# A windowed-attention block on one core: DVE, ACT and GpSimd do a step's work in another order

## The chip, the cores and the metric

The kernel runs on one core of one Trainium2 chip. The metric is the device time of one launch in microseconds (us), taken as the median of several runs. The kernel has five instruction streams: PE (matmul, with its weight loads shown apart as PEld), DVE (vector), ACT (scalar), POOL (GpSimd) and SP (which here only issues DMAs).

## What is computed

A Swin-like block over a float32 image batch of shape (4, 256, 256, 96), rolled by (-4, -4) and cut into 8x8 windows of 64 tokens. The reference, cut to what matters:

```
h = _ln(win, ln1_g, ln1_b)
q = jnp.einsum('ntc,chd->nthd', h, wq) + bq
k = jnp.einsum('ntc,chd->nthd', h, wk) + bk
v = jnp.einsum('ntc,chd->nthd', h, wv) + bv
scores = jnp.einsum('nqhd,nkhd->nhqk', q, k) * (1.0 / np.sqrt(KD))
attn = jax.nn.softmax(scores, axis=-1)
o = jnp.einsum('nhqk,nkhd->nqhd', attn, v)
win = win + jnp.einsum('nqhd,hdc->nqc', o, wo) + bo
h2 = _ln(win, ln2_g, ln2_b)
win = win + jax.nn.gelu(h2 @ w1 + b1, approximate=False) @ w2 + b2
```

There are 3 heads of 32 channels, and `_ln` is a layer norm over the 96 channels.

## The kernel before

**Tiling and stages.** The image is cut into 256 units of 1024 tokens (half a row of windows each). Sixteen units make a batch, and there are 16 batches. A batch is an attention stage of 16 steps and then an MLP stage of 16 units. Every unit stays in SBUF in `stream` from its load to its store.

**An attention step is a software pipeline over units.** In PE's step s (PE `attention_step`) these follow each other: the scores of unit s+1 (L645), the three transposes of unit s's probabilities, one per head (L660), the first half of the q and k projections of unit s+2 (L612, six matmuls), the product of probabilities and values (L675), the second half of q and k (L612), v (L629), and the output projection of unit s (L688). PE takes its instructions in order, so one that waits holds all behind it.

**The other engines in the same step.** DVE takes the row maxima (L1017) and subtracts them (L1024) head by head, sums the exponentials (L1032) and inverts the sums (L1040), all for unit s+1. Then it adds the attention output into `stream` (L1046) and takes the eight `bn_stats` of unit s for the second layer norm (L963, `statistics2`). ACT copies the transposed probabilities (L810), takes three exponentials (L821), copies q and k (L800, L804), o (L827) and v (L815) out of PSUM, and rounds each half of the normalised input of unit s+3 to fp32r (L792, `copy_hT_upper`). POOL subtracts that rounded half from the input to get the lower part (L398, `copy_hT_lower`), and multiplies the exponentials by the inverse sums (L391, `normalise_probs`, three instructions, one per head).

**What sets the order.** Each engine's order is written out by hand, and semaphores join them. POOL's step was: lower half 0, the three products, lower half 1, with statistics work (`finish1`, `finish2`: nine or ten small instructions), `normalise2` or `lower_early` ahead of it in some steps. The products of POOL's step s are read by the transposes of PE's step s+1, and the lower halves of POOL's step s are read by the q and k projections of the same PE step s+1: the first matmul there waits for half 0.

**The way of the normalised input.** ACT normalises unit u (`normalise1`, L781), DVE transposes it in blocks (`turn_h1`, L1010), SP sends it to DRAM (L301) and fetches it back in another layout (L309) for `copy_hT_upper`. SP waits in order: in its step s it sends unit s+4 and then fetches unit s+3. In batch 0 every step does this. In the later batches three steps do, and the rest of it falls into the MLP stage, except the fetch, which every step has.

Of the kernel before, what the change touches and what calls it, by code (L numbers as in the profile page):

```python
# [42 lines left out]
BATCH = 16  # L43
# [11 lines left out]
AHEAD = 3  # L55
# [13 lines left out]
def swin_block(nc, x, ln1_g, ln1_b, wq, bq, wk, bk, wv, bv, wo, bo, ln2_g, ln2_b, w1, b1, w2, b2, out):  # L69
# [3 lines left out]
    with ExitStack() as ctx:  # L73
# [306 lines left out]
        def _(pool):  # L380
# [146 lines left out]
            def attention(b):  # L527
                batch = b * BATCH
                call = LN_CALLS * (b - 1) + BATCH_0_CALLS
                for s in range(BATCH):  # L530
# [20 lines left out]
                    if s == 13:  # L551
                        lower_early(b, batch + 1, 1, copy_h2T_early(batch + 1, 1))
                    copy_hT_lower(batch + s + 3, (s + 3) % 2, 0)
                    normalise_probs(batch + s + 1, (s + 1) % 2)
# [214 lines left out]
        def _(act):  # L769
# [62 lines left out]
            def attention_step(u, half):  # L832
# [8 lines left out]
                if not absent(front):  # L841
                    copy_qk(front, 0)
                    copy_qk(front, 1)
                if not absent(middle):
                    exps(middle, 1 - half, 1)
# [5 lines left out]
                copy_hT_upper(u + 3, 1 - half, 0)  # L851
# [91 lines left out]
        def _(dve):  # L943
# [149 lines left out]
            def attention_step(u, half):  # L1093

                back, middle = u, u + 1
                if not absent(middle):
                    for h in range(HEADS):
                        maxima(middle, h)
                        shift(middle, 1 - half, h)
                    for h in range(HEADS):  # L1100
                        sums(middle, 1 - half, h)
                    invert_sums(middle)
                if not absent(back):
                    for g in range(2):
                        add_attention(back, g)

            def first_attention():

                for s in range(-5, BATCH):
                    if s >= -AHEAD:  # L1110
                        attention_step(s, s % 2)
                    if s >= 0:
                        statistics2(s, s)
# [3 lines left out]
                    if s + 8 < BATCH + AHEAD + 1:  # L1117
                        first_statistics(s + 8)
                    if s + 5 < BATCH + AHEAD:
                        turn_h1(s + 5, turned1_early)  # L1120
                    if s in (6, 8, 12):
                        n = (6, 8, 12).index(s)
                        turn_h2(n, turned_early, n == 0)

            TURNS1 = (9, 11, 13)
            TURNS2 = (5, 8, 10)

            def attention(b):
                batch = b * BATCH

                def whole_step(s):
                    attention_step(batch + s, s % 2)
                    statistics2(batch + s, s)

                wait_apart(dve, h1_left, 16 * (batch + BATCH))
                with dve.Fori(0, 1):
                    for s in range(6):
                        whole_step(s)
                        if 2 <= s < 3 + AHEAD:
                            n = s - 2  # L1140
                            statistics1(batch + BATCH + n, n, b * BATCH_ROWS + BATCH_ROWS + n // 2, n % 2)
                        if s == TURNS2[0]:
                            turn_h2(batch, turned_early, True)
                with dve.Fori(3, 4) as r:
                    for half in (0, 1):
                        attention_step(batch + 2 * r + half, half)
                        statistics2(batch + 2 * r + half, 2 * r + half)
                with dve.Fori(0, 1):
                    for s in range(8, 14):
                        whole_step(s)  # L1150
# [3 lines left out]
                        if s in TURNS2:  # L1154
                            n = TURNS2.index(s)
                            turn_h2(batch + n, turned_early, False)
                with dve.Fori(7, 8) as r:
                    for half in (0, 1):
                        attention_step(batch + 2 * r + half, half)
                        statistics2(batch + 2 * r + half, 2 * r + half)  # L1160
# [65 lines left out]
```

## Time and profile before

| what | value |
|---|---|
| median of 3 runs | 5030.46 us (5025.09 to 5032.2) |
| the profiled execution | 5033.9 us |
| its span, first to last instruction | 5029.7 us |
| mean granted TensorE clock | 0.998 |
| PE / PEld / DVE / ACT / POOL busy | 95% / 78% / 82% / 79% / 78% |

The views used are the page of the profile, the list of waits (who waited for whom, in total), and the timeline (instructions of an engine in order of time, runs of the same line merged into one row with their count). The timeline's times are us from the start of the span. A row starts with its start and its duration, and a bracket at its end is the idle time of the engine ahead of it and what ended that.

### The profile page before, as it was taken

To read this page: it belongs to the slowest core of one execution; us is meant where nothing else is said; L and a number is where in the kernel's file an instruction comes from. 1 tells how busy PE (TensorE), PEld (TensorE's weight loads), DVE (VectorE), ACT (ScalarE), POOL (GpSimd) and SP (SyncE) were. 2 spreads that over 40 slices of the span, in tenths; PEclk is the share of its full clock that TensorE was granted. 3 is DMA by queue.
4 is the path that set the end of the run, shared out by engine and by line. 5 is a ranking of instruction groups with operands and counts; after the bars stand their busy time and mean duration, and the time that the engine had idled before them with its cause. 6 is when DMAs were issued, how large, how long until landed. Compare 5 with 4: busy or idle time off the path is not lost.

```text
span 5029.7 us, 290167 instructions
## 1 busy us (share of the span) xinstructions
PE 4792.6 (95%) x109308; PEld 3899.6 (78%) x109308; DVE 4101.5 (82%) x9010; ACT 3953.4 (79%) x8309; POOL 3913.3 (78%) x4457
## 2 busy tenths in 40 slices
PE   5899999999999999999999999999999999999999
PEld 4687777878778787787877878778787777878777
DVE  7887878788787887878878788787887878888787
ACT  6887878777787777878778777787887878877787
POOL 6796868878687886878868688686896868878687
PEclk9999999999999999999999999999999999999999
DMA  4443443533434343343433434334343443533334
GB/s 124 116 160 94 124 136 93 171 96 123 128 101 161 95 138 117 103 160 97 138 112 109 155 91 150 105 117 148 101 154 95 127 135 97 168 99 123 126 100 163
DMA packets 374740, 622.61 MB, mean 124 GB/s; under 512 B 38761, under 2 KB 241226, under 8 KB 374282
## 3 DMA queue, kind: packets, MB, share of 16 engines
q1 hardware_dynamic: 372720, 618.28, 39.5%
q14 instruction: 449, 3.68, 0.2%
q10 hardware_dynamic: 1562, 0.50, 0.1%
q8 instruction: 9, 0.15, 0.0%
HBM read 310.35 MB, written 308.28 MB: 123 GB/s over the span
## 4 chain that ended last, share of the span: by engine, by line
PE 39%; DVE 16%; issue 14%; POOL 13%; ACT 8%; DMA 4%; SPq 3%; DVEq 3%; ACTq 0%; POOLq 0%
PE psum L722 12%; PE psum L736 11%; POOL probs L391 6%; PE psum L612 6%; DVE stats L963 4%; PE psum L629 3%; DVE normed L1067 3%; POOL rstd L430 2%; POOL hT_lower L398 2%; PE psum L688 2%; DVE stream L1046 2%; PE psum L675 2%; SPq L276 2%; DVE normed L1060 2%; DMA h_raw_odd<-turned_rows 2%
## 5 line engine op out<-in xcount | busy, mean ns | idle before, releaser
L781 ACT ACTIVATE normed<-stream,shift,rstd 128x96 f32 (+1 forms) x2176 | 809.8, 458 | 254.0 <-DVE probs L1010 241.2
L1046 DVE TENSOR_TENSOR stream<-stream,psum 128x384 f32 (+1 forms) x1024 | 562.8, 550 | 467.9 <-PE psum L736 226.5
L430 POOL TENSOR_TENSOR rstd<-variance,minus_half 128x16 f32<-128x16 f32 (+1 forms) x265 | 791.7, 2988 | 20.8
L398 POOL TENSOR_TENSOR hT_lower<-h_raw_odd,hT_upper 96x512 fp32r<-96x512 f32 x258 | 329.8, 1278 | 595.0 <-ACT hT_upper L792 591.1
L391 POOL TENSOR_TENSOR probs<-probs,prob_inv 128x512 f32<-128x512 f32 x771 | 781.8, 1040 | 0.0
L810 ACT ACTIVATE gelu_odd<-psum 128x512 f32<-128x512 f32 x768 | 424.4, 596 | 431.6 <-PE psum L660 426.0
L963 DVE BATCH_NORM_STATS2 stats<-stream 128x6 f32 (+2 forms) x4224 | 714.1, 243 | 42.0 <-DVE stream L1046 36.3
L821 ACT ACTIVATE probs<-probs 128x512 f32<-128x512 f32 x771 | 486.8, 631 | 122.7 <-DVE probs L1024 122.6
L736 PEld LDWEIGHTS psum<-w_w,gelu_odd 128*64 128x64 f32 x12288 | 511.2, 137 | 58.6 <-issue 58.6
L1024 DVE TENSOR_TENSOR probs<-psum,row_max 128x512 f32<-128x512 f32 x771 | 533.3, 692 | 26.6
L1032 DVE TENSOR_REDUCE prob_sum<-probs 128x8 f32<-128x512 f32 x771 | 492.0, 678 | 76.0 <-ACT probs L821 75.2
L736 PEld LDWEIGHTS psum<-w_w,gelu_even 128*64 128x64 f32 x12288 | 511.3, 137 | 51.2 <-issue 51.2
L736 PE MATMUL psum<-w_w,gelu_odd 128*64 128x96 f32 x12288 | 535.2, 247 | 12.2 <-ACT gelu_odd L865 12.2
L398 POOL TENSOR_TENSOR hT_lower<-h_raw_even,hT_upper 96x512 fp32r<-96x512 f32 x260 | 332.4, 1279 | 270.9 <-ACT hT_upper L792 269.9
L736 PE MATMUL psum<-w_w,gelu_even 128*64 128x96 f32 x12288 | 535.2, 247 | 3.3
L660 PE MATMUL psum<-ident,probs 128*128 128x128 f32 x3072 | 463.0, 284 | 78.5 <-POOL probs L391 59.4
L1017 DVE TENSOR_REDUCE row_max<-psum 128x8 f32<-128x512 f32 x771 | 521.1, 676 | 15.9 <-PE psum L645 15.8
L865 ACT ACTIVATE gelu_odd<-psum 128x512 f32<-128x512 f32 x768 | 428.6, 591 | 120.0 <-PE psum L722 93.3
L487 POOL TENSOR_TENSOR stream<-stream,b_all 128x768 f32 (+1 forms) x256 | 487.1, 1906 | 26.3 <-POOL rstd L430 25.3
L865 ACT ACTIVATE gelu_even<-psum 128x512 f32<-128x512 f32 x768 | 425.5, 590 | 79.5 <-PE psum L722 54.7
L612 PE MATMUL psum<-hT_upper,qk_split_upper 128*96 128x512 f32 x1032 | 449.9, 436 | 26.6 <-POOL hT_lower L398 23.0
L660 PEld LDWEIGHTS psum<-ident,probs 128*128 128x128 f32 x3072 | 325.4, 141 | 181.3 <-issue 163.0
(99 smaller groups left out, 11188.3 us busy)
## 6 DMA issues: line engine op xcount, KB each, us to landing
turned_rows<-probs SPq DMA_DIRECT2D x416, 384.0 KB, 2.4
h_raw_odd<-turned_rows SPq DMA_DIRECT2D x242, 384.0 KB, 3.9
stream<-in_x SPq DMA_DIRECT2D x272, 192.0 KB, 3.6
h_raw_even<-turned_rows SPq DMA_DIRECT2D x130, 384.0 KB
out<-stream SPq DMA_DIRECT2D x256, 192.0 KB
stream<-in_x SPq DMA_DIRECT2D x272, 180.0 KB
out<-stream SPq DMA_DIRECT2D x256, 180.0 KB
oT<-turned_rows SPq DMA_DIRECT2D x112, 384.0 KB
```

The source lines that it names most:

```text
L391: nc.gpsimd.tensor_tensor(block_h, block_h, inv, ALU.mult).then_inc(probs_ready, 1)
L398: nc.gpsimd.tensor_tensor(lower[:, tokens], h_raw[parity][0:C, tokens], upper[:, tokens], ALU.subtract).then_inc(hT_copied, 1)
L430: nc.gpsimd.tensor_tensor(flat(rstd), variance[:, 0:n], minus_half[:, 0:n], ALU.pow)\
L612: last = nc.tensor.matmul(psum[0:C, QK_BANKS[n], :], qk_split[w][:, which, :], hT_split[h][:, group * SHARES:(group + 1) * SHARES], start= ...
L660: last = nc.tensor.transpose(psum[:, PT_BANKS[h], quad * P:(quad + 1) * P], probs[:, buffer, h, 2 * quad:2 * quad + 2, :].rearrange("p a k ...
L722: last = nc.tensor.matmul(psum[:, UP_BANKS[part][j], :], w1_split[w][:, j * P:(j + 1) * P], h2T[parity][h][:, part * SHARES:(part + 1) * S ...
L736: last = nc.tensor.matmul(psum[WT * side:WT * (side + 1), DOWN_BANKS[part], t * C:(t + 1) * C], gelu[parity][:, j, c * P + WT * side:c * P ...
L781: last = nc.scalar.activation(normed1[:, t, :], stream[:, slot, t * C:(t + 1) * C], ACT.Identity, bias=shift1[:, index, t:t + 1], scale=rs ...
L865: nc.scalar.activation(in_rows[:, 2 * part:2 * part + 2, :, :], psum[:, UP_BANKS[part][j], :].rearrange("p (b t i) -> p b t i", b=2, i=BLOCK),
L963: last = nc.vector.bn_stats(stats[:, index, c, :], stream[:, slot, c * C:(c + 1) * C])
L1024: nc.vector.tensor_tensor(probs[:, buffer, h, :, :], psum[:, S_BANKS[h], :].rearrange("p (t k) -> p t k", k=WT), row_max[:, h, :].unsqueez ...
L1046: nc.vector.tensor_tensor(part, part, psum[:, banks[g], 0:GROUP], ALU.add).then_inc(added, 1)
```

## The change

DVE: `statistics2` of a unit leaves the end of its step and stands in the next step between the second and the third sum. The work that was done after it in some steps (`statistics1`, `turn_h1`, `turn_h2`) now stands behind the inversion and ahead of the two additions. In batch 0 the `statistics1` moves in this way and `turn_h1` and `turn_h2` stay at the step's end. The fourth `statistics1` of a batch moves from step 5 to step 6. ACT: `copy_hT_upper` of half 0 moves from behind the third exponential to behind the first two copies of q and k. POOL: the three products move ahead of lower half 0. The loops of DVE are cut in other places. Nothing is added or removed.

```
--- before.py
+++ after.py
@@ -550,8 +550,8 @@
                         finish2(call + 5, batch + 6, 6, 2)
                     if s == 13:
                         lower_early(b, batch + 1, 1, copy_h2T_early(batch + 1, 1))
+                    normalise_probs(batch + s + 1, (s + 1) % 2)
                     copy_hT_lower(batch + s + 3, (s + 3) % 2, 0)
-                    normalise_probs(batch + s + 1, (s + 1) % 2)
                     copy_hT_lower(batch + s + 3, (s + 3) % 2, 1)
                 return call + 6
 
@@ -841,6 +841,7 @@
                 if not absent(front):
                     copy_qk(front, 0)
                     copy_qk(front, 1)
+                copy_hT_upper(u + 3, 1 - half, 0)
                 if not absent(middle):
                     exps(middle, 1 - half, 1)
                 if not absent(back):
@@ -848,7 +849,6 @@
                     copy_oT(back, 1)
                 if not absent(middle):
                     exps(middle, 1 - half, 2)
-                copy_hT_upper(u + 3, 1 - half, 0)
                 if not absent(front):
                     copy_qk(front, 2)
                     copy_qk(front, 3)
@@ -1090,16 +1090,22 @@
                 dve.wait_ge(down_done, 2 * u + g + 1)
                 add_into_stream(u, DOWN_BANKS, g, mlp_added)
 
-            def attention_step(u, half):
+            def attention_step(u, half, index, extra=()):
 
                 back, middle = u, u + 1
                 if not absent(middle):
                     for h in range(HEADS):
                         maxima(middle, h)
                         shift(middle, 1 - half, h)
-                    for h in range(HEADS):
-                        sums(middle, 1 - half, h)
+                    sums(middle, 1 - half, 0)
+                    sums(middle, 1 - half, 1)
+                if not (isinstance(index, int) and index < 1):
+                    statistics2(u - 1, index - 1)
+                if not absent(middle):
+                    sums(middle, 1 - half, 2)
                     invert_sums(middle)
+                for work in extra:
+                    work()
                 if not absent(back):
                     for g in range(2):
                         add_attention(back, g)
@@ -1108,56 +1114,48 @@
 
                 for s in range(-5, BATCH):
                     if s >= -AHEAD:
-                        attention_step(s, s % 2)
-                    if s >= 0:
-                        statistics2(s, s)
+                        extra = [lambda: first_statistics(s + 8)] if s + 8 < BATCH + AHEAD + 1 else []
+                        attention_step(s, s % 2, s, extra)
+                    else:
+                        first_statistics(s + 8)
                     if s == -4:
                         for halves in h2T:
                             constant_rows(*halves)
-                    if s + 8 < BATCH + AHEAD + 1:
-                        first_statistics(s + 8)
                     if s + 5 < BATCH + AHEAD:
                         turn_h1(s + 5, turned1_early)
                     if s in (6, 8, 12):
                         n = (6, 8, 12).index(s)
                         turn_h2(n, turned_early, n == 0)
-
+                statistics2(BATCH - 1, BATCH - 1)
+
+            STATS1 = (2, 3, 4, 6)
             TURNS1 = (9, 11, 13)
             TURNS2 = (5, 8, 10)
 
             def attention(b):
                 batch = b * BATCH
 
-                def whole_step(s):
-                    attention_step(batch + s, s % 2)
-                    statistics2(batch + s, s)
-
-                wait_apart(dve, h1_left, 16 * (batch + BATCH))
-                with dve.Fori(0, 1):
-                    for s in range(6):
-                        whole_step(s)
-                        if 2 <= s < 3 + AHEAD:
-                            n = s - 2
+                def step(s):
+
+                    def extra():
+                        if s in STATS1:
+                            n = STATS1.index(s)
                             statistics1(batch + BATCH + n, n, b * BATCH_ROWS + BATCH_ROWS + n // 2, n % 2)
-                        if s == TURNS2[0]:
-                            turn_h2(batch, turned_early, True)
-                with dve.Fori(3, 4) as r:
-                    for half in (0, 1):
-                        attention_step(batch + 2 * r + half, half)
-                        statistics2(batch + 2 * r + half, 2 * r + half)
-                with dve.Fori(0, 1):
-                    for s in range(8, 14):
-                        whole_step(s)
                         if s in TURNS1:
                             n = TURNS1.index(s)
                             turn_h1(batch + BATCH + n, turned1_early)
                         if s in TURNS2:
                             n = TURNS2.index(s)
-                            turn_h2(batch + n, turned_early, False)
-                with dve.Fori(7, 8) as r:
-                    for half in (0, 1):
-                        attention_step(batch + 2 * r + half, half)
-                        statistics2(batch + 2 * r + half, 2 * r + half)
+                            turn_h2(batch + n, turned_early, n == 0)
+
+                    attention_step(batch + s, s % 2, s, (extra,))
+
+                wait_apart(dve, h1_left, 16 * (batch + BATCH))
+                for part in (range(0, 6), range(6, 11), range(11, BATCH)):
+                    with dve.Fori(0, 1):
+                        for s in part:
+                            step(s)
+                statistics2(batch + BATCH - 1, BATCH - 1)
 
             def mlp(b):
                 batch_row = b * BATCH_ROWS
```

**DVE in batch 0**, from the additions of one step to the inversion of the next (`gelu_even` is the buffer that `turn_h1` writes). Before:

```order
L1046 TENSOR_TENSOR stream<-stream,psum 128x384 x2
L963 BN_STATS stats<-stream 128x6 x16
L1010 STREAM_TRANSPOSE gelu_even<-normed 128x8x24x4
L1017 TENSOR_REDUCE row_max<-psum 128x8
...
L1024 TENSOR_TENSOR probs<-psum,row_max 128x512
L1032 TENSOR_REDUCE prob_sum<-probs 128x8 x3
L1040 RECIPROCAL prob_inv<-prob_sum 128x24
```

Now:

```order
L1046 TENSOR_TENSOR stream<-stream,psum 128x384 x2
L1010 STREAM_TRANSPOSE gelu_even<-normed 128x8x24x4
L1017 TENSOR_REDUCE row_max<-psum 128x8
...
L1024 TENSOR_TENSOR probs<-psum,row_max 128x512
L1032 TENSOR_REDUCE prob_sum<-probs 128x8 x2
L963 BN_STATS stats<-stream 128x6 x8
L1032 TENSOR_REDUCE prob_sum<-probs 128x8
L1040 RECIPROCAL prob_inv<-prob_sum 128x24
L963 BN_STATS stats<-stream 128x6 x8
```

Eight of the sixteen `bn_stats` went between the sums, and eight behind the inversion. In the later batches the eight of `statistics2` do the same.

**POOL at the start of a later batch's attention.** Before:

```order
L398 TENSOR_TENSOR hT_lower<-h_raw_odd,hT_upper 96x512
L387 REGISTER_ALU
L391 TENSOR_TENSOR probs<-probs,prob_inv 128x512 x3
L397 REGISTER_ALU
L398 TENSOR_TENSOR hT_lower<-h_raw_odd,hT_upper 96x512
```

Now:

```order
L391 TENSOR_TENSOR probs<-probs,prob_inv 128x512 x3
L397 ISA
L398 TENSOR_TENSOR hT_lower<-h_raw_odd,hT_upper 96x512
L397 REGISTER_ALU
L398 TENSOR_TENSOR hT_lower<-h_raw_odd,hT_upper 96x512
```

The three products went ahead of lower half 0, and both halves now follow the third product.

**ACT in one step of batch 0**, from the copies of the transposed probabilities to the normalisation. Before:

```order
L810 ACTIVATE gelu_odd<-psum 128x512 x3
L821 ACTIVATE probs<-probs 128x512
L800 ACTIVATE qT<-psum 96x128x4
L804 ACTIVATE kT<-psum 96x16x32
L821 ACTIVATE probs<-probs 128x512
L827 ACTIVATE oT<-psum 96x8x16x4 x2
L821 ACTIVATE probs<-probs 128x512
L792 ACTIVATE hT_upper<-h_raw_odd 96x512
```

Now:

```order
L810 ACTIVATE gelu_odd<-psum 128x512 x3
L821 ACTIVATE probs<-probs 128x512
L800 ACTIVATE qT<-psum 96x128x4
L804 ACTIVATE kT<-psum 96x16x32
L792 ACTIVATE hT_upper<-h_raw_odd 96x512
L821 ACTIVATE probs<-probs 128x512
L827 ACTIVATE oT<-psum 96x8x16x4 x2
L821 ACTIVATE probs<-probs 128x512
```

The rounding of half 0 went ahead of two exponentials and two copies. PE's and SP's orders are unchanged.

## Rows read from the trace of the kernel before

**Rows 1.** The page: busy time of each engine.
```profile
PE 4792.6 (95%) x109308; PEld 3899.6 (78%) x109308; DVE 4101.5 (82%) x9010; ACT 3953.4 (79%) x8309; POOL 3913.3 (78%) x4457
```

**Rows 2.** Waits of all engines: us in total, times, longest us.
```profile
POOL hT_lower L398 <- ACT hT_upper L792: 861.0, 222, 23.0
...
PE psum L660 <- POOL probs L391: 59.4, 174, 1.6
...
ACT hT_upper L792 <- DMA h_raw_odd<-turned_rows: 30.9, 44, 5.1
```

**Rows 3.** Timeline of PE, step 1 of batch 4: start, duration, instruction.
```profile
1328.13 0.89 PE L645 MATMUL psum<-kT,qT 32*64 32x64 f32 x61
...
1330.82 0.47 PE L612 MATMUL psum<-hT_upper,qk_split_upper 128*96 128x512 f32 x1
...
1332.06 0.40 PE L612 MATMUL psum<-hT_lower,qk_split_upper 128*96 128x512 f32 x1
...
1338.00 1.29 PE L645 MATMUL psum<-kT,qT 32*64 32x64 f32 x96
```

**Rows 4.** Timeline of PE: batch 4's first scores, and its MLP's first matmul.
```profile
1318.27 0.97 PE L645 MATMUL psum<-kT,qT 32*64 32x64 f32 x67 [0.42 <-issue]
...
1488.04 0.47 PE L722 MATMUL psum<-h2T_even_upper,w_split_upper 128*128 128x512 f32 x1
```

**Rows 5.** Timeline of PE, a step of batch 4: third transposes, first q projection.
```profile
1405.23 0.65 PE L660 MATMUL psum<-ident,probs 128*128 128x128 f32 x4 [0.35 <-POOL probs L391]
...
1405.70 0.44 PE L612 MATMUL psum<-hT_upper,qk_split_upper 128*96 128x512 f32 x1
```

**Rows 6.** Timeline of POOL, the same step.
```profile
1402.07 3.03 POOL L391 TENSOR_TENSOR probs<-probs,prob_inv 128x512 f32<-128x512 f32 x3
...
1405.07 1.27 POOL L398 TENSOR_TENSOR hT_lower<-h_raw_even,hT_upper 96x512 fp32r<-96x512 f32 x1
```

**Rows 7.** Timeline of ACT, the same step.
```profile
1407.41 0.58 ACT L804 ACTIVATE kT<-psum 96x512 f32<-96x512 f32 x1
...
1407.89 0.63 ACT L821 ACTIVATE probs<-probs 128x512 f32<-128x512 f32 x1
...
1409.43 0.62 ACT L821 ACTIVATE probs<-probs 128x512 f32<-128x512 f32 x1
1409.95 0.62 ACT L792 ACTIVATE hT_upper<-h_raw_odd 96x512 fp32r<-96x512 f32 x1
1410.47 0.59 ACT L800 ACTIVATE qT<-psum 96x512 f32<-96x512 f32 x1
```

**Rows 8.** Timeline of DVE, the same step.
```profile
1403.12 1.38 DVE L963 BATCH_NORM_STATS2 stats<-stream 128x6 f32 x8 [0.15 <-DVE stream L1046]
...
1408.38 1.27 DVE L1032 TENSOR_REDUCE prob_sum<-probs 128x8 f32<-128x512 f32 x2
...
1410.08 0.69 DVE L1032 TENSOR_REDUCE prob_sum<-probs 128x8 f32<-128x512 f32 x1 [0.43 <-ACT probs L821]
...
1410.80 0.30 DVE L1040 RECIPROCAL prob_inv<-prob_sum 128x24 f32<-128x24 f32 x1
```

**Rows 9.** Timeline of batch 0: PE's scores 13 steps apart (first and last row), normalisation to rounding.
```profile
61.49 1.54 PE L645 MATMUL psum<-kT,qT 32*64 32x64 f32 x96 [3.09 <-issue]
...
158.38 2.99 ACT L781 ACTIVATE normed<-stream,shift,rstd 128x96 f32<-128x96 f32 x8
...
161.40 0.98 DVE L1010 STREAM_TRANSPOSE gelu_even<-normed 128x768 f32<-128x768 f32 x1 [0.36 <-ACT normed L781]
...
163.02 0.35 SPq L309 DMA_DIRECT2D h_raw_odd<-turned_rows  x1
...
167.33 0.63 ACT L792 ACTIVATE hT_upper<-h_raw_odd 96x512 fp32r<-96x512 f32 x1
...
218.34 1.28 PE L645 MATMUL psum<-kT,qT 32*64 32x64 f32 x96 [0.79 <-ACT v L815]
```

**Rows 10.** Windows, batch 0: us; busy PE, PEld, DVE, ACT, POOL; granted clock; DMA.
```profile
220.00:225.00 5.00, 3.11 (x15) 2.37 (x16) 3.12 (x5) 3.60 (x9) 5.00 (x6) 0.78 0.25 79
```

## Prediction

> **What bounds the kernel now.** The page first [rows 1]: PE is busy for 95% of the span, so that a faster order has at most the last few per cent of it to win, and all other engines have about a fifth of their time free. In such a kernel the question is which chain holds PE up inside a step. The MLP stage has the same instructions in the same order after the change, so I read the attention steps alone.
>
> The list of waits [rows 2] shows PE's third transposes waiting for POOL's products 174 times, 59.4 us in all. POOL itself waited 861 us for ACT's rounded half before it could do the lower half. Both are what the change moves. So next the timeline of PE in one step. Step 1 of batch 4 [rows 3] runs without a wait: scores at 1328.13, the first q projection at 1330.82 (2.69 later), the next scores at 1338.00, which is a step of 9.87 us. From the first q projection to the next scores it is 7.18 us. Call the moment of that first projection Q. A step then lasts (Q measured from its scores) + 7.18, and nothing is won below 9.87.
>
> The whole attention stage of batch 4 goes from 1318.27 to 1488.04 [rows 4], 169.8 us for 16 steps, 10.61 a step. The most that the change can win is therefore 0.74 x 16 = 11.9 us a batch, 190 us in all. In a later step of it [rows 5, 6] POOL's third product ends at 1405.10, the third transposes start 0.13 later, and Q is 0.47 behind them: Q is 0.60 after the end of the third product. I call that end E.
>
> **The change, part by part.**
>
> *POOL's order.* The products no longer stand behind a lower half that takes 1.27 [rows 6]. But PE's first q projection needs that lower half, and in the same PE step as the products. It now starts at E - 0.03 and ends at E + 1.24, and with the handoff of 0.13 Q is at E + 1.37 in place of E + 0.60. So the products come up to 1.2 us earlier and 0.77 of it goes into a new wait of PE, at L612 on L398. What is queued behind the waiting matmul is all of the step that is left.
>
> *ACT's order.* The rounding of half 0 starts 0.52 ahead of what follows it (1409.95 to 1410.47) [rows 7], so the second and third exponentials come 0.52 later after the copies of q and k.
>
> *DVE's order.* The eight `bn_stats` take 1.38 [rows 8] and no longer stand ahead of the maxima, which now start when the scores are done. That is worth nothing once the chain of the exponentials, which runs through ACT, ends later than the subtractions. Between the second and third sum they cost what they exceed DVE's wait there: it was 0.43 of idle time [rows 8], and with both exponentials late by the same amount some 0.4 of the `bn_stats` stay uncovered. The other moved work (`statistics1`, the turns) goes into the time after the inversion, where DVE waits for the output projection. I cost it at nothing: it has about a microsecond of room there, and if that is gone the additions, and with them the transposes that need their banks, come late by tenths.
>
> *The new loop.* These close into a loop from E of one step to E of the next. In us after E:
> - Q at 1.37, as above.
> - Six matmuls to the end of the last, 1332.06 + 0.40 - 1330.82 = 1.64 [rows 3], and about 0.03 of handoff, as from an exponential's end at 1410.05 to its sum at 1410.08 [rows 7, 8]: the copy of k starts at 3.04.
> - The rounding 0.48 later (3.52), the second exponential 0.52 after that (4.04), 0.63 long, handoff 0.03: its sum at 4.70.
> - The next DVE instruction starts 0.59 later, since two sums take 1.27 and not 1.36. The `bn_stats` start at 5.29 and let the third sum start, overlapped in the same way, at 6.59.
> - The third exponential is ready before that: four ACT starts behind the rounding, 2.06 less the 0.04 overlaps, its end is near 6.1. So the third sum waits for DVE, not for ACT.
> - Inversion 0.72 later, 0.30 long [rows 8]: 7.61.
> - Handoff to POOL, which no row shows: between 0.03 and 0.13. I take 0.10, between the two. Three products, 3.03 [rows 6]: E again after **10.75 us**.
>
> In the loop nothing has slack, so the step is 10.75 wherever it has settled. Between the end of lower half 1 (two halves after E, 2.5) and the next products (7.7) POOL has 5.2 us in which its statistics work lies hidden; if it should not fit, six steps of a batch are late by tenths, which the bounds take in. The normalisations of three steps of a batch, 3 us of ACT each, stay hidden as far as ACT waits for the transposes anyway; I cost them at nothing, and if that cover is gone they too are tenths.
>
> *A later batch.* Step 0 starts with everything ready, 9.87. Its own inversion has no `bn_stats` in it, so step 1 is about 10.5. Fourteen of 10.75 are 150.5. Sum 170.9, against 169.8: **+1.1 us**, times 15 batches **+17 us**. The steps that were longest before (with sixteen `bn_stats` ahead of the maxima) get shorter, and the plain ones get longer. For the bounds: if the handoffs and overlaps of the loop are 0.2 shorter it is -25 us, if 0.25 longer +70.
>
> *Batch 0.* Here every step has a second loop: normalisation (2.99), turn (starts 161.40), then SP sends, then fetches (163.02), and the rounding starts at 167.33, 4.3 after the fetch [rows 9]. In this batch ACT reached the rounding only a moment before the data, and steps are (218.34 - 61.49) / 13 = 12.07 us. Now ACT comes to the rounding 2.06 us earlier in its order (1407.89 to 1409.95) [rows 7], but the data are no earlier, since SP's fetch stands behind a send that waits for the turn. ACT stands still with two exponentials and two copies behind it, and these 2.06 us then lie between the rounding and the next normalisation. The loop becomes 14.1. Fourteen steps of it: **+29 us**. The bounds are nothing (the fetch lands in time after all) and the same again.
>
> [...]
>
> **Sum.** 5033.9 + 17 + 29 = 5080 for an execution like the profiled one. That one was 3.4 above the median of the runs, so 5076 is the forecast.
>
> **The rivals.**
>
> *A. Faster: PE does not wait for the lower half.* If E comes early enough in the step (1.32 or less after the scores, so that Q stays at 2.69), the earlier maxima decide. It needs the inversion 0.9 us earlier than my loop gives from an undisturbed Q. For it speaks that DVE starts the maxima up to 1.3 us earlier, and that PE waited for POOL 174 times. Against it, the second exponential stands on ACT behind the copy of k, which no earlier maximum moves. With steps of 10.0, a batch is 160, -9.8 x 15 = -147, and with batch 0's +29 the median is 4912. In a half form (a loop of 10.5, and half of batch 0's cost) it is 5033.9 - 36 + 15 - 3.4 = 5010. The two together 0.16.
>
> *B. Batch 0 costs nothing*, because the fetch lands before ACT gets there: 5047. Against it, ACT already waited for that DMA 44 times [rows 2]. 0.08.
>
> *C. The clock.* PE will wait nearly a microsecond in each step (10.75 - 9.87). In batch 0 the granted clock was 0.78 in the mean of a stretch of 5 us in which PE was busy for only 3.11 of them [rows 10], so at half its rate for 2.2 us, which loses about 1.1. One such dip in every fifth of 15 x 14 steps would give 42 x 1.1 = +46, near 5122, and one in every second step +115, near 5190. Against it, the mean granted clock of the whole span is 0.998, with steps of 12 us in batch 0. 0.07. The Trainium skill, TensorE: Matmul & The Clock Gate, section A second HAM failure mode, says that short idles between matmul groups can let the clock swing between its levels; rows of this case show one such stretch in batch 0 and none for the later batches I looked at.
>
> *D. No difference*: PE is at its own pace and both effects are small, 5030. 0.07, since loops do bind here.
>
> **How the numbers follow.** The forecast has 0.62, A 0.16, B 0.08, C 0.07, D 0.07. A measurement of this kernel tells 0.2%, 10 us, from no change. A is faster; D and a little of the forecast's lower edge are within 0.2%; the rest is slower. That gives 0.17, 0.09 and 0.74. The forecast's own range is 5035 to 5110, from the bounds of the loop (-25, +70, not both with batch 0's). The range for 8 in 10 is 5025 to 5125: it takes in B and D, leaves out A and most of C.
>
> **What would show it.** In the profile after: a new wait of PE at L612 on POOL's L398 in most attention steps, while the wait at L660 shrinks; steps that are all alike at 10.7 to 10.8, and no gain beyond step 1; `bn_stats` that delay the third sum; in batch 0 ACT's L792 waiting for the DMA about 2 us a step, and steps near 14. It is wrong if later batches' steps fall well below 10.5, which would mean that the second exponential is earlier than ACT's order lets me think, or if batch 0 stays at 12.

## The result and the profile after

The changed kernel takes **5073.26 us** (median of 4 runs, 5066.04 to 5078.03) against 5030.28 us in the same measurement: ratio 1.0086, 95% interval 1.0068 to 1.0103. It is slower by 0.9%, clear of the 0.2% that a measurement can tell. The profiled execution took 5066.04 us, the lowest of the four, with a span of 5061.7 us, 32.0 more than before.

The page of the changed kernel, busy time of each engine [rows 1]:

```profile
PE 4790.0 (95%) x109308; PEld 3908.6 (77%) x109308; DVE 4113.9 (81%) x9010; ACT 3964.6 (78%) x8309; POOL 3912.5 (77%) x4457
```

No engine has more work. The time went into waits. The list of waits of the changed kernel (us in total, times, longest us) answers to [rows 2]:

```profile
POOL probs L391 <- DVE prob_inv L1040: 868.1, 226, 24.1
...
PEld psum L612 <- POOL hT_lower L398: 164.7, 225, 0.7
PE psum L612 <- POOL hT_lower L398: 133.1, 226, 22.1
...
POOL hT_lower L398 <- ACT hT_upper L792: 49.8, 19, 9.3
...
ACT hT_upper L792 <- DMA h_raw_even<-turned_rows: 25.6, 13, 10.4
ACT hT_upper L792 <- DMA h_raw_odd<-turned_rows: 21.9, 11, 5.1
...
PE psum L660 <- POOL probs L391: 6.3, 20, 0.4
```

PE's wait for the products is nearly gone (59.4 us before), and in its place PE's first q projection waits for the lower half 225 times: in every attention step of the 15 later batches but the first. Before the change that wait had been seen once. POOL's own large wait has only changed its name: it waited for ACT's rounding, and now it waits for the inversion.

The new loop in one step of batch 4, on PE, POOL, ACT and DVE in this order (timeline):

```profile
1426.84 1.57 PE L660 MATMUL psum<-ident,probs 128*128 128x128 f32 x12
1428.90 0.47 PE L612 MATMUL psum<-hT_upper,qk_split_upper 128*96 128x512 f32 x1 [0.50 <-POOL hT_lower L398]
...
1436.08 1.13 PE L645 MATMUL psum<-kT,qT 32*64 32x64 f32 x83
```
```profile
1425.57 2.05 POOL L391 TENSOR_TENSOR probs<-probs,prob_inv 128x512 f32<-128x512 f32 x2
1427.58 2.53 POOL L398 TENSOR_TENSOR hT_lower<-h_raw_even,hT_upper 96x512 fp32r<-96x512 f32 x2
...
1435.21 3.04 POOL L391 TENSOR_TENSOR probs<-probs,prob_inv 128x512 f32<-128x512 f32 x3 [0.33 <-DVE prob_inv L1040]
```
```profile
1430.57 0.59 ACT L804 ACTIVATE kT<-psum 96x512 f32<-96x512 f32 x1
1431.06 0.62 ACT L792 ACTIVATE hT_upper<-h_raw_odd 96x512 fp32r<-96x512 f32 x1
1431.58 0.62 ACT L821 ACTIVATE probs<-probs 128x512 f32<-128x512 f32 x1
```
```profile
1432.23 0.69 DVE L1032 TENSOR_REDUCE prob_sum<-probs 128x8 f32<-128x512 f32 x1 [0.75 <-ACT probs L821]
1432.84 1.37 DVE L963 BATCH_NORM_STATS2 stats<-stream 128x6 f32 x8
1434.11 0.68 DVE L1032 TENSOR_REDUCE prob_sum<-probs 128x8 f32<-128x512 f32 x1
1434.82 0.30 DVE L1040 RECIPROCAL prob_inv<-prob_sum 128x24 f32<-128x24 f32 x1
```

The third product ends at 1427.62, and the next step's third product at 1435.21 + 3.04 = 1438.25, which is 10.63 later. Everything on the way follows the one before it with no more than 0.1 us between: lower half, q projection (1.28 after the product's end), k copied, rounding, second exponential, its sum, eight `bn_stats`, third sum, inversion, products.

Here is where the span's 32 us are. The numbers are differences of the starts of the scores rows in each kernel's timeline; those of the later batches are means over 15 of them for the steps and over 14 for the last column.

| us | batch 0, first 16 scores intervals | steps 0 to 14 of a later batch | its step 15 and MLP |
|---|---|---|---|
| before | 196.2 | 159.4 | 149.4 |
| changed | 219.5 | 159.0 | 150.5 |

Batch 0 gives +23.3. A later batch gives -0.4 in its attention and +1.05 behind it, 15 times +0.6, which is +9. Steps 1 to 14, which were 9.9 to 11.6 us long before, are now nearly all 10.6, and their sum is nearly the same.

In batch 0 PE's clock fell too. The windows view of one stretch of it (us; busy PE, PEld, DVE, ACT, POOL; granted clock; DMA), before and changed:

```profile
80.00:240.00 160.00, 140.56 (x4160) 104.37 (x4147) 141.30 (x369) 142.66 (x318) 128.26 (x162) 0.99 0.40 113
```
```profile
80.00:240.00 160.00, 127.14 (x3686) 99.88 (x3673) 123.20 (x339) 125.11 (x279) 111.86 (x143) 0.93 0.35 97
```

Between the two levels of 2.4 and 1.2 GHz, 0.93 is about 22 of the 160 us at the lower one, against 3 before. Timeline of PE at the end of batch 0's longest step in the changed kernel, and the windows view there:

```profile
209.46 1.51 PE L629 MATMUL psum<-qkv_w,h_raw_even 128*32 128x96 f32 x32 [3.71 <-ACT oT L827]
210.90 2.83 PE L688 MATMUL psum<-wo_w,oT 128*64 128x96 f32 x32
```
```profile
208.00:214.00 6.00, 4.54 (x82) 4.04 (x88) 4.77 (x21) 6.00 (x15) 3.82 (x4) 0.50 0.17 35
```

PE had waited 3.71 us for ACT, and the output projection (L688) took 2.83 us at a granted clock of 0.50, where the next step's took 1.54. From 400 to 5000 us the granted clock is 1.00 in both kernels.

### The profile page after: what moved, and what is told of

It is laid out like the page before. It is cut to its first block, busy times and chain, and to the rows that moved or that the text cites. A ratio compares the mean times of both kernels' runs of the same rounds, so it can differ in the third digit from the quotient of the medians.

```text
span 5061.7 us, 290182 instructions
## 1 busy us (share of the span) xinstructions
PE 4790.0 (95%) x109308; PEld 3908.6 (77%) x109308; DVE 4113.9 (81%) x9010; ACT 3964.6 (78%) x8309; POOL 3912.5 (77%) x4457
## 4 chain that ended last, share of the span: by engine, by line
POOL 30%; issue 25%; PE 19%; DVE 10%; DMA 4%; ACT 4%; SPq 4%; DVEq 2%; POOLq 1%; ACTq 0%
POOL hT_lower L398 10%; POOL probs L391 9%; PE psum L722 9%; PE psum L736 7%; POOL rstd L430 4%; DVE normed L1067 3%; DMA turned_rows<-probs 3%; SPq L276 3%; DVE normed L1060 2%; DVE stats L963 2%; PE psum L612 1%; POOL normed L462 1%; ACT normed L781 1%; POOL normed L458 1%; DMA h_raw_odd<-turned_rows 1%
## 5 line engine op out<-in xcount | busy, mean ns | idle before, releaser
L810 ACT ACTIVATE gelu_odd<-psum 128x512 f32<-128x512 f32 x768 | 409.7, 598 | 475.8 <-PE psum L660 475.5
L1046 DVE TENSOR_TENSOR stream<-stream,psum 128x384 f32 (+1 forms) x1024 | 545.1, 545 | 277.9 <-PE psum L736 209.4
L1032 DVE TENSOR_REDUCE prob_sum<-probs 128x8 f32<-128x512 f32 x771 | 522.6, 678 | 215.9 <-ACT probs L821 215.9
L865 ACT ACTIVATE gelu_odd<-psum 128x512 f32<-128x512 f32 x768 | 429.5, 591 | 120.7 <-PE psum L722 93.0
L487 POOL TENSOR_TENSOR stream<-stream,b_all 128x768 f32 (+1 forms) x256 | 486.1, 1901 | 27.2 <-POOL rstd L430 25.3
L660 PE MATMUL psum<-ident,probs 128*128 128x128 f32 x3072 | 422.3, 281 | 20.8 <-POOL probs L391 6.3
L612 PE MATMUL psum<-hT_lower,qk_split_upper 128*96 128x512 f32 x1032 | 409.4, 397 | 0.0
L612 PE MATMUL psum<-hT_upper,qk_split_lower 128*96 128x512 f32 x1032 | 407.1, 394 | 0.0
L688 PE MATMUL psum<-wo_w,oT 128*64 128x96 f32 x8192 | 399.0, 251 | 0.0
```

What stands on the lines that cost most here:

```text
L612: last = nc.tensor.matmul(psum[0:C, QK_BANKS[n], :], qk_split[w][:, which, :], hT_split[h][:, group * SHARES:(group + 1) * SHARES], start= ...
L865: nc.scalar.activation(in_rows[:, 2 * part:2 * part + 2, :, :], psum[:, UP_BANKS[part][j], :].rearrange("p (b t i) -> p b t i", b=2, i=BLOCK),
L1032: nc.vector.tensor_reduce(prob_sum[:, h, :], probs[:, buffer, h, :, :], AXIS.X, ALU.add).then_inc(sum_step, 1)
L1046: nc.vector.tensor_tensor(part, part, psum[:, banks[g], 0:GROUP], ALU.add).then_inc(added, 1)
```

## The experiments

The ten kernels compute all of the output. Each was timed beside the kernel before on the same chip; between the four measurements the median of before moved from 5030 to 5035, so that absolute times compare to some 5 us.

| run | what differs | median us | ratio to before, 95% |
|---|---|---|---|
| changed | all three parts | 5073.3 | 1.0086 (1.0068 to 1.0103) |
| e1 | DVE and ACT parts | 4987.5 | 0.9906 (0.9889 to 0.9922) |
| e2 | DVE part alone | 4925.5 | 0.9783 (0.9767 to 0.9799) |
| e3 | changed, ACT old in batch 0 | 5042.9 | 1.0018 (1.0008 to 1.0027) |
| e4 | changed, `bn_stats` behind the inversion | 5064.4 | 1.0057 (1.0040 to 1.0074) |
| e5 | DVE and POOL parts | 4970.1 | 0.9868 (0.9852 to 0.9884) |
| e6 | POOL part alone | 5032.8 | 0.9991 (0.9982 to 1.0001) |
| e7 | ACT part alone | 5207.7 | 1.0341 (1.0323 to 1.0358) |
| e8 | changed, POOL old in each later batch's last step | 5058.0 | 1.0047 (1.0030 to 1.0063) |
| e9 | changed, `turn_h1` behind the additions | 5130.8 | 1.0194 (1.0177 to 1.0212) |
| e10 | DVE part alone, of it only `statistics2` | 4928.7 | 0.9795 (0.9779 to 0.9812) |

**e1: POOL's order undone.**

```
                     if s == 13:
                         lower_early(b, batch + 1, 1, copy_h2T_early(batch + 1, 1))
-                    normalise_probs(batch + s + 1, (s + 1) % 2)
                     copy_hT_lower(batch + s + 3, (s + 3) % 2, 0)
+                    normalise_probs(batch + s + 1, (s + 1) % 2)
                     copy_hT_lower(batch + s + 3, (s + 3) % 2, 1)
```

> The changed kernel with POOL's old order (lower half 0, products, lower half 1); ACT and DVE as changed. My theory (a loop in which PE waits for a lower half that stands behind the products): PE's wait at L612 on L398 goes, plain steps of the later batches fall from 10.64 to about 10.0, steps with finish1 or finish2 stay near 10.6 since POOL's own work fills them, and the MLP stage gives back its 1.1 us a batch: about 4970 us. Rival (the bn_stats between the sums are what costs): steps stay at 10.4 or more, about 5050.

4987.5 us: 86 less than the changed kernel. The waits of e1 no longer have PE waiting for the lower half beyond the start of the program:

```profile
PE psum L660 <- POOL probs L391: 50.0, 149, 0.4
...
PE psum L612 <- POOL hT_lower L398: 21.7, 1, 21.7
```

Steps 3, 5, 7 are 9.95 us and steps 4, 6, 8 are 10.6 to 10.7, and the stretch behind the attention is back at 149.5. So the lower half behind the products is what held the later batches at 10.63 in every step. The gain was 17 us smaller than expected, because steps 2, 12 and 14, which have no `finish` work before them, stay at 10.4.

**e2: DVE's part alone.** Both POOL's and ACT's orders are undone, POOL's as in e1, and in ACT:

```
                 copy_qk(front, 1)
-                copy_hT_upper(u + 3, 1 - half, 0)
...
                     exps(middle, 1 - half, 2)
+                copy_hT_upper(u + 3, 1 - half, 0)
```

> Only DVE's part of the change; POOL and ACT as before. My theory: the inversion comes at about 6.4 us after the end of the third product of the step before and the lower half is done with it, so plain steps run at 9.9, steps with finish at 10.6, and batch 0 returns to 12.1 a step (-23 us): about 4930 us, faster than both kernels. Rival (the bn_stats between the sums are what costs): no faster than before, 5030 or more.

4925.5 us, as expected, and faster than both kernels by 2.2% and 2.9%. Batch 0 is back (194.8), and a later batch's 15 steps take 152.3 us. What is left are the steps behind POOL's `finish1` or `finish2` (10.5 to 10.7); the others run at 9.8 to 10.0. Its page:

```profile
PE 4748.7 (97%) x109308; PEld 3897.5 (79%) x109308; DVE 4103.7 (83%) x9010; ACT 3924.3 (80%) x8309; POOL 3899.3 (79%) x4457
```

**e3: ACT's old order in batch 0 alone.** `copy_hT_upper` stands in both places, the first under `if not isinstance(u, int)` and the second under `if isinstance(u, int)`; only batch 0's units are plain numbers.

```
+                if not isinstance(u, int):
+                    copy_hT_upper(u + 3, 1 - half, 0)
-                copy_hT_upper(u + 3, 1 - half, 0)
...
+                if isinstance(u, int):
+                    copy_hT_upper(u + 3, 1 - half, 0)
```

> The changed kernel with ACT's old order in batch 0 alone. My theory (in batch 0 ACT stands still for the fetched input with two exponentials and two copies behind it): batch 0 returns to steps near 12.1, 23 us less, about 5050 us, and nothing else moves. Rival (batch 0 is longer because of DVE's new order): no more than 5 us less.

5042.9 us, 30 less by the medians and 19 less by the spans. Batch 0's steps are 12.09 us again, after 13.68 in the changed kernel, and its 16 intervals take 196.6 us (196.2 before). So ACT's order, and not DVE's, made batch 0 longer. The granted clock between 80 and 240 us is back at 0.99 as well, so this run takes away ACT's wait and the lower clock together.

**e4: the `bn_stats` behind the inversion.**

```
-                if not (isinstance(index, int) and index < 1):
-                    statistics2(u - 1, index - 1)
                 if not absent(middle):
                     sums(middle, 1 - half, 2)
                     invert_sums(middle)
+                if not (isinstance(index, int) and index < 1):
+                    statistics2(u - 1, index - 1)
```

> The changed kernel with the eight bn_stats of statistics2 behind the inversion and not between the second and the third sum. My theory: the inversion comes 0.4 us earlier, plain steps fall from 10.64 to 10.25; steps with finish stay at 10.6; where statistics1 also stands there the additions come late and cost some tenths: 5010 to 5040 us. Rival (the lower half behind the products holds PE whatever DVE does): steps stay at 10.6, about 5073 us.

5064.4 us, only 9 less by the medians and 1 less by the spans; the intervals of the two ratios overlap. Both readings missed. Step 3 does fall to 10.25, so the 0.4 us of `bn_stats` on the loop are real, but the additions now come late, and PE's first transposes wait for them in most steps:

```profile
1386.86 1.00 DVE L1046 TENSOR_TENSOR stream<-stream,psum 128x384 f32 x2
```
```profile
1387.46 1.53 PE L660 MATMUL psum<-ident,probs 128*128 128x128 f32 x12 [0.96 <-DVE stream L1046]
```

The list of waits has 82.0 us of this in 140 waits, which the changed kernel did not have, and the DMA's wait at L792 rises from 21.9 to 60.6 us because the turns come later too. What was saved between the sums was given back behind the inversion.

**e5: DVE and POOL, ACT as before.** The edit of ACT is that of e2, with POOL as changed.

> DVE's and POOL's parts of the change, ACT as before. My theory: the loop through the lower half stays, but without ACT's rounding ahead of the second exponential it is 0.5 us shorter: PE waits at L612 on L398 as in the changed kernel, plain steps 10.15, steps with finish 10.6; batch 0 at 12.1 a step; the MLP stage keeps its 1.1 us: about 4995 us. Rival (ACT's rounding is hidden in the later batches and costs only in batch 0): steps stay at 10.64, about 5043 us.

4970.1 us. Steps 3, 5 and 7 are 10.12 to 10.15, as the shorter loop says, those with `finish` 10.5 to 10.6, and the part behind the attention keeps about half of its extra time (150.0). The total is lower than my figure of 4995, because I had summed it wrongly: from the same step lengths it comes out near 4980. The rival is out, ACT's rounding does lie on the loop of the later batches.

**e6: POOL's part alone.** The three-line swap of e1, the other way round, in the kernel before.

> Only POOL's part of the change; DVE and ACT as before. My theory: steps are set in turn by the maxima that start behind the bn_stats and by the lower half behind the products, which do not add up in full: 10.25 in plain steps, 10.6 to 10.9 in those with finish or with sixteen bn_stats, +1.1 in each MLP stage, batch 0 unchanged: 4990 to 5040 us. Rival (POOL's order costs by itself what the changed kernel lost): 5050 or more.

5032.8 us, no difference (0.9991, 0.9982 to 1.0001). This lies in the range that I gave, but not for my reasons. With DVE's maxima late the steps are as before, 159.6 us for fifteen (steps 3, 5 and 7 at 10.5 to 10.6, not 10.25), although the weight loads of the q projection wait for the lower half 212 times (111.9 us). The part behind the attention is 149.5 as before, so POOL's order alone does not bring the extra 1.1 us there either. POOL's order costs nothing as long as another loop is slower, and in DVE's presence it costs what e5 has over e2, 45 us.

**e7: ACT's part alone.** The ACT lines of the change in the kernel before.

> Only ACT's part of the change; DVE and POOL as before. My theory: batch 0 costs its 23 to 29 us; in the later batches the lower half is done well ahead of the inversion, POOL's wait of 861 us on the rounding shrinks, and the exponentials are 0.5 later: steps 0.1 to 0.3 shorter, 5010 to 5040 us. Rival (the rounding on POOL's way did not matter): 5053 or more.

5207.7 us, 3.4% slower: a clear miss. Batch 0 is 35 us longer (231.6), and 150 us come from three steps of each later batch, 10, 12 and 14, which take 14.9, 13.7 and 14.2 us. Timeline of ACT, and below it of SP, in one of them:

```profile
1493.07 0.58 ACT L804 ACTIVATE kT<-psum 96x512 f32<-96x512 f32 x1
1496.56 0.63 ACT L792 ACTIVATE hT_upper<-h_raw_odd 96x512 fp32r<-96x512 f32 x1 [2.91 <-DMA h_raw_odd<-turned_rows]
1497.09 0.61 ACT L821 ACTIVATE probs<-probs 128x512 f32<-128x512 f32 x1
```
```profile
1491.11 0.38 SPq L301 DMA_DIRECT2D turned_rows<-gelu_even  x1
1492.06 0.37 SPq L309 DMA_DIRECT2D h_raw_odd<-turned_rows  x1
```

PE's timeline in the same step, with the output projection of the step before in the first row, and the windows row:

```profile
1486.06 1.54 PE L688 MATMUL psum<-wo_w,oT 128*64 128x96 f32 x32
...
1498.72 1.32 PE L629 MATMUL psum<-qkv_w,h_raw_even 128*32 128x96 f32 x32 [3.19 <-ACT oT L827]
1499.98 2.69 PE L688 MATMUL psum<-wo_w,oT 128*64 128x96 f32 x32
```
```profile
1499.00:1502.00 3.00, 3.00 (x56) 2.72 (x48) 1.23 (x3) 3.00 (x8) 1.68 (x2) 0.50 0.08 14
```

This is batch 0's loop in another place. In these steps SP's fetch stands behind a send that waits for `turn_h1`, the turn ran behind the additions and `bn_stats`, and ACT stood idle for 2.91 us with two exponentials behind it. PE, which waited 3.19 us for ACT, then ran at half its clock, and the output projection took 1.15 us more than the step before. The granted clock of the whole run is 0.982, and 35 of these 45 steps hold such a stretch. At 1.15 us each that would be some 40 of the 150 us, by an estimate; no run takes the clock apart from the wait. The changed kernel does not show it, and the theory that followed was that DVE's early turn is what hides it.

**e9: the turn put back, in the changed kernel.**

```
                     def extra():
...
-                        if s in TURNS1:
-                            n = TURNS1.index(s)
-                            turn_h1(batch + BATCH + n, turned1_early)
...
                     attention_step(batch + s, s % 2, s, (extra,))
+                    if s in TURNS1:
+                        n = TURNS1.index(s)
+                        turn_h1(batch + BATCH + n, turned1_early)
```

> The changed kernel with turn_h1 of the three steps of each later batch behind the additions, where it was before. Theory formed after the ACT-only run (ACT's new order is harmless in the later batches only because the turn is ahead of the additions, so that SP's send and the fetch behind it are done when ACT gets there): in the three steps the fetch lands about 1.7 us after ACT wants it, 75 us more, about 5150 us, with ACT's wait at L792 on the DMA well over 100 us. Rival (the ACT-only kernel lost its time to late maxima): within 15 us of 5073.

5130.8 us, 57 more than the changed kernel. Steps 10 to 14 rise from 10.6 or 10.7 to between 11.2 and 11.8 (3.5 us a batch, 52 in all), and ACT's wait on the fetch of the odd units from 21.9 us to 73.9:

```profile
ACT hT_upper L792 <- DMA h_raw_odd<-turned_rows: 73.9, 49, 4.8
```

Direction and place are as the theory says. The size is three quarters of what I gave, and ACT's wait on both fetches comes to 100 us where I gave well over that. The granted clock of the later batches is 1.00 here, so its 57 us come without a lower clock. How e7's other 90 us or so divide between the late maxima, the longer wait and the lower clock is not shown.

**e8: the last step of each later batch.**

```
+                    if s < BATCH - 1:
+                        normalise_probs(batch + s + 1, (s + 1) % 2)
-                    normalise_probs(batch + s + 1, (s + 1) % 2)
                     copy_hT_lower(batch + s + 3, (s + 3) % 2, 0)
+                    if s == BATCH - 1:
+                        normalise_probs(batch + s + 1, (s + 1) % 2)
                     copy_hT_lower(batch + s + 3, (s + 3) % 2, 1)
```

> The changed kernel with POOL's old order in the last attention step of each later batch alone. My theory (POOL starts its MLP work 1.3 us later, because both lower halves stand behind the last products, and DVE's first normalisation there runs against it): the MLP stage gives back about 1 us a batch, 15 us less, about 5058 us. Rival (the MLP stage is longer because of DVE's late bn_stats): unchanged, about 5073 us.

5058.0 us, 15 less by the medians (8.6 by the spans). The part behind the attention falls from 150.5 to 150.0 on average, but the averages hide a cleaner picture: a few batches of each kernel are 1 to 2.5 us shorter than the rest, and step 15 is in this number. From the first matmul of the MLP stage to the next batch's first scores, the median of 14 batches is 139.2 us before, 140.2 in the changed kernel and 139.2 in e8. So the MLP stage gives back all that it had gained, and POOL's order in the last step is the cause. In the batch that I looked at, PE's gap of 0.74 us in the second unit of the MLP stage is gone. POOL's order is not enough by itself: the same number is 139.4 in e6 (POOL alone) and 139.9 in e5 (DVE and POOL).

**e10: of DVE's part only `statistics2`.**

```
-                for work in extra:
-                    work()
                 if not absent(back):
                     for g in range(2):
                         add_attention(back, g)
+                for work in extra:
+                    work()
```

> DVE's part of the change alone, and of it only the move of statistics2 between the sums: statistics1 and the turns go back behind the additions; POOL and ACT as before. Theory: statistics2 is what stood ahead of the maxima in every step, so that it alone gives most of the gain; the nine steps of a batch with other work there keep a late start: 4940 to 4965 us. Rival (the gain comes from statistics1 and the turns, which were the longest): 5000 or more.

4928.7 us, the same as e2 within their intervals, and faster than the 4940 that I gave at best: the steps with other work at their end do not start late enough to matter (152.7 us for fifteen steps, 152.3 in e2). The eight `bn_stats` taken from ahead of the maxima give all of DVE's gain; the earlier turns and `statistics1` give none where ACT has its old order, and the earlier `turn_h1` gives 57 us where ACT and POOL have the new ones (e9).

## Why the prediction was right, and where not

The forecast was 5076 us and slower; it is 5073. The two causes that it named are the two that were found, and each is shown by a run that takes it away.

- **The loop through the lower half: right.** Its length was given as 10.75, and it is 10.63. Term by term after the third product's end: q projection 1.28 (1.37 forecast: the handoff from POOL to PE is 0.05 here, and I had taken 0.13 from the transposes), copy of k 2.95 (3.04), rounding 3.44 (3.52), second exponential 3.96 (4.04), its sum 4.61 (4.70), `bn_stats` 5.22 (5.29), third sum 6.49 (6.59), inversion's end 7.50 (7.61), products 7.59. The handoff to POOL, which no row had shown, is 0.09 (0.10). All the rest was right to 0.03, so the error is mostly that one handoff, some 0.1 us in 14 x 15 steps.
- **A later batch: the size came near by two errors of opposite sign.** I gave +1.1 us, and it is +0.6. Its attention steps are in fact 0.4 shorter, as the loop is 0.1 shorter than forecast. But the sentence that failed is "the MLP stage has the same instructions in the same order after the change, so I read the attention steps alone": the MLP stage is 1.0 us longer. POOL enters it with two lower halves behind the last products where it had one, and e8, which changes only that, has the old length again.
- **Batch 0: right in cause, a little large.** Forecast steps of 14.1 and +29 us, measured 13.68 and +23. ACT's wait was 0.9 to 2.9 us where the timeline shows it, 1.9 in the mean of 14 steps and so near the 2.06. But the steps grew by 1.6 only, and a part of that may be the clock, which the term did not have: the same code of batch 0 takes 219.5 us in the changed kernel at a granted clock of 0.93 (80 to 240 us), and 220.7, 220.8 and 223.7 in e1, e8 and e9 at 0.90, 0.89 and 0.89. By these an estimate of the clock's share is 2 to 6 of the 23 us; it is not isolated. (In batch 0 POOL's order is unchanged; the change touches it in the later batches only. The term did not rest on it.)

Timeline of ACT in one step of batch 0 after the change, to be held against [rows 9]:

```profile
164.09 0.58 ACT L804 ACTIVATE kT<-psum 96x512 f32<-96x512 f32 x1
165.59 0.63 ACT L792 ACTIVATE hT_upper<-h_raw_even 96x512 fp32r<-96x512 f32 x1 [0.92 <-DMA h_raw_even<-turned_rows]
166.13 0.61 ACT L821 ACTIVATE probs<-probs 128x512 f32<-128x512 f32 x1
```

- **The other moved work of DVE, costed at nothing: right as a sum, wrong as a reading.** I looked at its room behind the inversion alone. It also carries ACT's new order: without the early turn the later batches would pay batch 0's price in three steps (57 us in e9; 150 in e7, where the clock fell as well). The wait of an engine that the text did not follow in the later batches, SP, decides there.
- **The sum.** Spans give +32 where I had +46; the medians give +43. The profiled execution is the lowest of its four, and both terms were too large (+17 for +9, +29 for +23), so the forecast's closeness to the median is in part luck.
- **Rivals.** A, PE not waiting for the lower half, did not happen, but e2 shows that its mechanism is real where POOL keeps its old order: the earlier maxima then give 2.2%. B is out by batch 0's +23.3, and D by the loop of 10.63 and by a time that is 0.9% longer. C did not happen where it was priced, in the later batches, whose granted clock is 1.00. In batch 0 it did: 0.93 for 0.99, after waits of PE that the change made longer (up to 3.71 us in this stretch, 1.56 before).

## What to carry to other kernels

When two operations of one engine feed the same consumer, ask in which order the consumer needs the last of them: moving the "urgent" one first only helps if the other is not needed right behind it. Moving an operation that waits on a DMA to an earlier place in an in-order engine puts all that it jumped over behind that DMA. And try the parts of a change apart: here one part alone was worth -2.2%, and the two others took 3% back. They do not add up either: on top of DVE's part, POOL's costs 45 us, ACT's 62 and both together 148.

## What was not expected of the hardware

**DVE and POOL hold each other up at the start of the MLP stage.** DVE's first normalisation there (L1060, 768 elements a partition, both inputs in SBUF) takes 0.94 to 0.96 us as its shortest and its median in the trace. Timeline of DVE and of POOL, kernel before:

```profile
1490.30 3.56 DVE L1060 TENSOR_TENSOR normed<-stream,mean 128x768 f32<-128x768 f32 x1
1493.89 2.48 DVE L1067 TENSOR_TENSOR normed<-normed,rstd 128x768 f32<-128x768 f32 x1
```
```profile
1489.95 1.29 POOL L398 TENSOR_TENSOR hT_lower<-h_raw_even,hT_upper 96x512 fp32r<-96x512 f32 x1
1491.20 4.36 POOL L487 TENSOR_TENSOR stream<-stream,b_all 128x768 f32 x2
```

And in the changed kernel:

```profile
1513.06 4.79 DVE L1060 TENSOR_TENSOR normed<-stream,mean 128x768 f32<-128x768 f32 x1
1517.88 2.54 DVE L1067 TENSOR_TENSOR normed<-normed,rstd 128x768 f32<-128x768 f32 x1
```
```profile
1512.67 2.55 POOL L398 TENSOR_TENSOR hT_lower<-h_raw_even,hT_upper 96x512 fp32r<-96x512 f32 x2
1515.18 4.34 POOL L487 TENSOR_TENSOR stream<-stream,b_all 128x768 f32 x2
```

The same DVE instruction took 0.94 (the shortest), 3.56 and 4.79 us, and in these two places POOL's instructions, which read SBUF as well, ran without a pause beside it. DVE's pair took 6.04 us together before and 7.33 after. In e8 (where the line is L1063), with one lower half fewer behind the products, it is 6.28 together, so the pair is what to look at and not its first instruction:

```profile
1512.87 5.32 DVE L1063 TENSOR_TENSOR normed<-stream,mean 128x768 f32<-128x768 f32 x1
1518.23 0.96 DVE L1070 TENSOR_TENSOR normed<-normed,rstd 128x768 f32<-128x768 f32 x1
```
```profile
1513.74 3.64 POOL L487 TENSOR_TENSOR stream<-stream,b_all 128x768 f32 x2
```

POOL was held up too: its two additions (L487) took 4.36 and 4.34 us here and 3.64 in e8. This fits what the Trainium skill, SBUF — State Buffer, section Who interferes with whom, says: a DVE instruction with two SBUF inputs contends with a GpSimd instruction that reads SBUF, because its second input comes through the shared read interface. The timelines agree with it; no run here isolates it. In the attention steps nothing of the kind is seen: POOL's products take 1.03 to 1.06 us at any place, beside DVE instructions with a PSUM input or a single one.

**Short waits of PE in every step left its clock alone; behind longer ones it fell.** In the later batches of the changed kernel PE is idle for half a microsecond in each step of 10.6 us, and the granted clock is 1.00. In batch 0 of the same kernel and in e7's long steps a wait of 3.71 and one of 3.19 us were followed by a stretch at a granted clock of 0.50, in which the output projection took 2.83 and 2.69 us for 1.54. Not every such wait was followed by one, and no run isolates what makes the clock fall.
